# Giving a gather slot back two groups later in the sum passes, and spline weights in SBUF instead of PSUM

## The reference

```python
# layer 0, spline: 8 weights per edge from 3 attributes, times the source row, times W[8]
z = (B[:, :, None] * xj[:, None, :]).reshape(Etot, S * x.shape[1])      # xj = h[src], S = 8
agg = segment_sum(z @ W.reshape(S * 64, 64), dst) / max(cnt, 1); out = agg + h @ root; batchnorm; elu
# layer 1, attention: alpha from leaky_relu(x_l[src] + x_r[dst]) @ att, softmax over the edges of a node
# layer 2, three convolutions: h = relu(dinv * segment_sum((h @ W * dinv)[src], dst) + self + b)
# layer 3: agg = segment_sum(h[src], dst) / max(deg, 1); out = concat([agg, h]) @ W.T + b
```

## Time and profile before

| | |
|---|---|
| median of 3 executions | 12690.88 us (12641.61 to 12698.97) |
| the profiled execution | 12644.07 us, its span 12642.2 us |
| mean granted TensorE clock | 0.793 of full speed |
| PE busy | 8810.2 us (70%) |
| VectorE (DVE) busy | 4847.3 us (38%) |
| GpSimd (POOL) busy | 7247.4 us (57%) |
| ScalarE (ACT) busy | 1810.1 us (14%) |
| spline pass | about 159 to 3840 us of the span |
| attention pass | about 4115 to 7690 us |
| four sum passes | about 7846 to 8968, 9062 to 10177, 10270 to 11390 and 11474 to 12575 us |

### The profile page before, as it was taken

The page is one execution under the profiler, slowest core; times in us unless marked ns, Lnnn a source line. Parts: engine busy times, 40 slices in busy tenths (PEclk is TensorE's granted clock), DMA queues, the critical chain, the costliest instruction groups (busy, mean ns, idle before and its releaser), DMA issues.

```text
span 12642.2 us, 197864 instructions
## 1 busy us (share of the span) xinstructions
PE 8810.2 (70%) x46558; PEld 6095.1 (48%) x46559; DVE 4847.3 (38%) x11847; ACT 1810.1 (14%) x4731; POOL 7247.4 (57%) x6848
## 2 busy tenths in 40 slices
PE   4787777778784666666667764788378747864885
PEld 4787777777774444555555553222222222221222
DVE  5554444444446233333333334222322232234223
ACT  0000000000001233333333332000000000000000
POOL 3446665655554776666666662556455545664664
PEclk8888888888886677777777786888588868876887
DMA  7401111111111322222222221444244424433443
GB/s 286 155 17 14 14 13 13 13 13 13 12 12 25 62 61 60 59 60 58 57 56 56 56 54 38 146 148 150 57 149 151 137 77 146 154 115 105 149 153 90
DMA packets 577485, 1013.05 MB, mean 80 GB/s; under 512 B 342921, under 2 KB 352440, under 8 KB 577331
## 3 DMA queue, kind: packets, MB, share of 16 engines
q1 hardware_dynamic: 258819, 724.21, 17.0%
q0 software_dynamic: 316112, 286.92, 12.9%
q10 hardware_dynamic: 2400, 0.53, 0.0%
HBM read 862.36 MB, written 148.79 MB: 80 GB/s over the span
## 4 chain that ended last, share of the span: by engine, by line
PE 34%; another core or an unknown queue 31%; issue 15%; DVE 7%; DVEq 4%; DMA 3%; ACT 3%; SPq 1%; ACTq 1%; POOL 0%; POOLq 0%
PE psAB L800 13%; PE psCD L910 4%; PE psCD L909 4%; DMA R<-dense 2%; PE psCD L808 2%; PE psAB L853 2%; PE psCD L866 2%; PE psAB L859 1%; DVE one_hot L1118 1%; PE psCD L844 1%; ACT Q L702 1%; PE psAB L850 1%; PE psCD L781 1%; PE psAB L893 1%
## 5 line engine op out<-in xcount | busy, mean ns | idle before, releaser
L544 POOL DMA_INDIRECT gath<-sum_tab,idx_block x2688 | 2669.2, 993 | 2201.8 <-issue 1154.8
L800 PE MATMUL psAB<-one_hot,R 128*128 128x128 f32 x15680 | 2424.4, 316 | 633.6 <-DVE one_hot L1118 317.0
L800 PEld LDWEIGHTS psAB<-one_hot,R 128*128 128x128 f32 x15680 | 2254.6, 221 | 707.7 <-issue 658.2
L544 POOL DMA_INDIRECT gath<-spline_tab,idx_block x1568 | 1502.0, 958 | 1542.0 <-DVEq L1051 1058.1
L544 POOL DMA_INDIRECT gath<-gat_tab,idx_block x1568 | 1541.2, 983 | 1023.2 <-DVEq L1051 579.7
L909 PE MATMUL psCD<-R,Q 128*128 128x512 f16 x3528 | 1505.2, 427 | 563.3 <-DMA R<-dense 493.7
L518 POOL DMA_INDIRECT dense<-count_block,cell_block x900 | 1496.3, 1663 | 424.2 <-issue 268.8
L910 PE MATMUL psCD<-R,Q 128*64 128x512 f16 x3528 | 1555.3, 441 | 17.2 <-issue 17.1
L1343 DVE SCALAR_TENSOR_TENSOR R<-iota_row,tile_base,dstf 128x512 f32 x928 | 705.1, 760 | 1168.3 <-issue 1168.3
L893 PE MATMUL psAB<-gath,R 128*128 128x192 bf16 x3712 | 508.2, 276 | 822.7 <-DVE R L1343 406.6
L1324 DVE TENSOR_REDUCE row_part<-psAB 128x64 f32 x940 | 331.7, 353 | 1855.9 <-PE psAB L893 756.8
(11 more groups left out here) (252 smaller groups left out, 9263.1 us busy)
## 6 DMA issues: line engine op xcount, KB each, us to landing
R<-dense SPq DMA_DIRECT2D x504, 896.0 KB
dense<-stage SPq DMA_DIRECT2D x126, 896.0 KB
Q<-dst_rows SPq DMA_DIRECT2D x392, 256.0 KB
gath<-sum_tab,idx_block POOLq DMA_INDIRECT x2688
gath<-spline_tab,idx_block POOLq DMA_INDIRECT x1568
gath<-gat_tab,idx_block POOLq DMA_INDIRECT x1568
sum_tab<-Q SPq DMA_DIRECT2D x28, 672.0 KB, 5.5
dense<-count_block,cell_block POOLq DMA_INDIRECT x900
```

The source lines that it names most:

```text
L544: nc.gpsimd.indirect_dma_start(out=dest[:, s, j, :], out_offset=None, in_=table, in_offset=bass.IndirectOffsetOnAxis(ap=idx_block[:, c:c + ...
L800: nc.tensor.matmul(block, z[:, w, j, k * P:(k + 1) * P], oh32[:, j, :], start=(j == 0), stop=(j == J - 1))
```

## The change

The change has two parts. In the four sum passes VectorE frees at the end of group g the slot of group g-6 instead of g-4, so GpSimd may issue at that moment the gathers of group g+2. The counts that GpSimd waits for are adapted: slots 2 to 7 take the extra count in the sum passes, held in a register of its own, `sums`. The spline and attention passes keep a lag of 4. In the spline pass `hat8` moves from PSUM to SBUF, to a free stretch of the tile `R`.

```diff
+        hat8 = R[:, o + 4 * J:o + 12 * J].rearrange("p (j a b) -> p j a b", a=2, b=4)
-        o += 4 * J
+        o += 12 * J
...
-        hat8 = psB[:, 0:KS * J].rearrange("p (j a b) -> p j a b", a=2, b=4)
...
         LAG = 4
+        SUM_LAG = 6
...
-            def edge_loop(table, dest, first, last, cells=None):
+            def edge_loop(table, dest, first, last, cells=None, extra=None):
...
                             if s >= LAG:
                                 pool.reg_add(pool_count, pool_count, pool_early)
+                            if extra is not None and s >= S - SUM_LAG:
+                                pool.reg_add(pool_count, pool_count, extra)
...
-                pool.reg_add(pool_early, pool_early, 1)
-                edge_loop(sum_tab, gath_sum, first_block, NBLK // 2)
+                pool.reg_add(sums, sums, 1)
+                edge_loop(sum_tab, gath_sum, first_block, NBLK // 2, extra=sums)
...
-                    give_back(s)
+                    free_slot((s - SUM_LAG) % S)
...
-                for s in range(LAG):
-                    give_back(s)
+                for s in range(SUM_LAG):
+                    free_slot((s - SUM_LAG) % S)
```

More of the change, by code:

```diff
@@ L579, in _ @@
             _, first_block = dense_range(pool, "pool")
+            (sums,) = registers(pool, "pool_sums", 1)
             with pool.Fori(0, 3) as layer:
```

## The result

The changed kernel took 12249.01 us (median of 4 runs, 12234.41 to 12289.06), the kernel before 12694.67 us (median of 4, 12641.61 to 12698.97): a ratio of 0.9663, 95% interval 0.9629 to 0.9698. I had forecast 12790 us in a range of 12680 to 12900. The change made it 3.4% faster, and the forecast was wrong in sign.

What follows compares the result with a forecast made beforehand. The prediction took PE's chain of waits as the bound, with GpSimd mattering only through late gathers. Part 1 gave 0, chunk ends 92 and tails 32, rounded to +120 us on a mean of 12669: 12790 us, range 12680 to 12900.

Steps and rivals of the forecast that it cites:

- What bounds the kernel: Whole kernel: PE has 34% of the chain of waits; GpSimd, busy 57%, matters only if a gather comes late.
- Part 1 (a): Spline pass, writing hat8 to SBUF instead of PSUM: at most 24 ns a group faster, 9 us in all.
- (b): Spline pass, product z with hat8 in SBUF: keeps its 2286 ns, no gain or loss.
- (d): Spline pass, GpSimd delaying VectorE operations with two SBUF inputs: at most 76 ns a group, bound 30 us.
- Part 1 (c): Spline pass, z stopping gathers by up to 2.29 us a group: covered, cost 0; without cover up to 898 us.
- Part 2: Sum passes, lag of 6: gathers come late where PE has groups without panels, 92 + 32 = 124, rounded to +120 us.
- the 36 stretches: Sum passes, chunk ends of 4 groups without panels: gathers 0 to 8.0 us late, together 138 us, two thirds counted, 92.
- the tails: Last 16 groups of each sum pass: gathers 7.6 us late at the end, 4 passes x 8 = 32 us.
- the delay is hidden: Rival, 0.22: in the sum passes PE's waits for one-hot matrices take in most late gathers; +0 to +60 us, 12700.
- faster: panels sooner: Rival, 0.07: fewer gathers in flight cut PE's panel waits by a quarter, -123 us; half the late gathers make it 12600.
- z held by GpSimd: Rival, 0.03: in the spline pass z waits out a gather that started before it, 110 us on top, 12900.
- the spline pass of the same length: Sign named for a right forecast: spline and attention passes keep their lengths, each sum pass 25 to 40 us longer.

Runs made afterwards that it cites:

- the run on record: First measured run of the whole change against the kernel before: 12249.01 us against 12694.67, ratio 0.9663.
- before_again: The kernel before itself, unchanged, run again with a trace in the third group: ratio 0.9999 to before at 10223.31 us.
- third group: Runs of the kernel before, the change and its halves, before at 10223.31 us: whole change 1.0585, hat8 in SBUF alone 1.0472, lag of 6 alone 1.0099.
- the first group: Runs of the halves and of GpSimd pauses, before at 12435.94 us: hat8 in SBUF alone 0.9735, lag of 6 alone 0.998, pauses in the kernel before 0.9663.
- groups two to five: Later groups of follow-up runs, with the kernel before at 10209.13 to 10223.31 us and no PE update late.
- pauses alone: The kernel before, hat8 in PSUM and lag 4, with a 128x128 GpSimd memset behind every gather of all passes: 0.9663.
- more_vector: The kernel before with one VectorE product of 896 elements more behind z in each spline-pass group: 1.0097, repeated at 1.0103 and 1.0105.

## Why the prediction was wrong, step by step

**What bounds the kernel.** "GpSimd sets no end; what it does matters only if a gather comes too late" failed. It was true of its data and not of its side effect: where PE's updates are held, GpSimd's rhythm sets when VectorE, ScalarE and the panels' loads go on. The sign of it was in the first row that I read, 31% of the chain put down to an unknown releaser in a program on one core. The prediction does not speak of it.

**Part 1 (a), (b), (d).** hat8 fell from 199 to 192 ns (I said 175 to 199), z went from 2286 to 2292 ns (I said it would keep its length), and one at most lasted 73 ns over the median. Right, all three, and all three small.

**Part 1 (c), the term that failed.** "Cost 0", with the stops covered by a lead of 14 to 30 us (it is 14.0 to 37.6, over 30 in 27 groups, which changes nothing). The stops came as described: gathers up to 3088 ns, 478 us of them in the run on record. Their worth was wrong twice over. Where updates are held, each stop breaks up a row of gathers and lets PE's updates through: -389 us between the traces, -338 us with hat8 alone. Where none is held, the cover that I counted isn't there. It was the idle time of a GpSimd ahead of a held-up PE: 10.06 us a group in the earlier trace rows, and 7.56 us over the same 280 groups in before_again, against the 7.4 us that I had worked out for GpSimd's own work and the 9.7 us with the stops (9.06 measured). There the stops cost 484 us. My own sentence gave that price: "without the cover it would be up to 898 us".

**Part 2.** The test by group, the 36 stretches and the tails gave +120 us. In the third group, with nothing held, the lag alone cost 3886 - 3765 = 121 us in the sum passes and 101 us in all. The sum was right there, in part by luck: the comparison by group was made in a trace where PE waited for gathers 14 times, at the starts of passes, while before_again, with the same lag of 4, has 121 such waits, most of them inside a pass. The lag of 6 added 30 waits and 82 us to them; what makes up the rest of the 121 us is not singled out. In the run on record the late gathers came as forecast (77 more waits, I said some 60; 276 us, I said 150 to 250) and the passes did not get longer: the rival "the delay is hidden" was the right one, 0.998 for the lag alone. It also named the cover, VectorE's one-hot matrices; the panels gave nearly as much. Both waits are in part made of held updates (lateness in the sum passes 2375 us before, 2026 after). Why the sum passes came out 32 us shorter rather than even, I did not single out.

**The rival "faster: panels sooner"** (0.07) had the right sign, and panels were waited for 89 us less, where it had put 123; but the late gathers took that up, and the gain was in the spline pass, of which it said nothing. **"z held by GpSimd"** fell, with z within 73 ns. The attention pass kept its length, as said; "the spline pass of the same length" was the observation that proved the forecast wrong.

**What stays open.** What sets whether updates are held: the two runs on record and the first group showed it, groups two to five did not, and the first and the last two groups report the same chip number. Within a group it never changed.

The traces differ in two more ways. The six held ones have only about a quarter of the updates that the gathers' DMAs make (22950 to 26779 of 5824 x 16 = 93184; 92097 in before_again), so that signals or their records are lost or merged there. No run tells which, nor whether tracing has a part in it. And the mean granted clock is 0.793 before and 0.865 in before_again, with PE busy for 8810 and 7975 us: 836 of the 2424 us between the two are PE's own slower work. A slower clock can't put four updates 0.05 us apart behind work of 0.33 us each, but whether it is only a consequence of the waiting no run shows. By what path GpSimd's gathers hold an update of PE, no run shows either.

That z's stops, rather than fewer reads of PSUM, give hat8's part of the gain was shown from one side only: pauses alone took as much off the whole with hat8 still in PSUM, but in the spline pass they gave 204 us where hat8 gave 338, and the other 134 may be better placed breaks or something else. Against fewer reads of PSUM stand the 3410 and 3414 us with pauses. In groups two to five PE's updates were on time with hat8 read from PSUM. The test from VectorE's side (more_vector) never met a held case. In the held case the best kernel run was the changed one with pauses everywhere (0.9628, within its interval the same as pauses alone); where nothing is held, none beat the kernel before.

## What to carry to other kernels

Account for every large share of the chain before weighing a change; behind "unknown" on a single core here were signals far behind their work, and the semaphore updates' times showed it. A measured slack is only as firm as what makes it: here the lead of GpSimd was another engine's lateness, and a 3.4% gain turned into a 5.9% loss where that was gone. A VectorE product with two SBUF inputs took 1.3 us a group from GpSimd's gathers at 2.29 us in one piece (513 / 392) and 0.46 us in two (1689.5 - 1509.9 = 180 us, / 392); where GpSimd is the bound, put one input in PSUM, or cut the product in pieces of about a gather's length.

## What the runs showed of the hardware that I had not expected

In some groups of runs PE's semaphore updates came up to 18 us after the matmul (the kernel before) while GpSimd issued indirect gathers 1.25 us apart; VectorE's and ScalarE's, in the spline and attention passes, were not seen late. A GpSimd memset of 0.22 us behind each gather, 0.09 us more between starts, took 3.4% off the kernel then and added 5.3% otherwise. The same program on the same kind of chip took 12.7 and 12.4 ms where updates were held and 10.2 ms where they were not.
